# Edge groups from 22 on, not 29, take normalised source rows from a table; 13 groups of them as the node stage ends

## The reference, cut to what matters

```
h = relu(layernorm(x))                                  # every node
em = relu(layernorm([h[src], h[dst]] @ msg_w + msg_b) * msg_g + msg_beta) * edge_weight
messages = mean of em over the edges with the same target (0 where there is none)
gate = sigmoid(h @ gate_w + gate_b)
h_new = relu(layernorm([h, messages] @ upd_w + upd_b) * upd_g + upd_beta)
out = x + gate * h_new + (1 - gate) * h
```

## Time and profile before

| | us |
|---|---|
| median of three runs | 986.97 |
| lowest and highest run | 982.22, 993.64 |
| the profiled execution | 981.87 |
| its span, first to last instruction | 980.1 |

### The profile page before, as it was taken

How to read it: one execution, slowest core, us unless ns; L and a number is a source line. 1 busy time by engine, 2 the same in 40 slices (tenths; PEclk the granted TensorE clock), 3 DMA queues, 4 the chain that set the end, 5 groups by cost and what they waited for, 6 DMA issues and landing times.

```text
span 980.1 us, 19229 instructions
## 1 busy us (share of the span) xinstructions
PE 698.9 (71%) x3696; PEld 547.5 (56%) x3696; DVE 873.4 (89%) x3834; ACT 852.0 (87%) x3678; POOL 673.0 (69%) x602
## 2 busy tenths in 40 slices
PE   2377787877777777886766377777867878687781
PEld 1255555555555555554555266666756766576661
DVE  7299999999989999999995379999998888879984
ACT  3299999999989999999996389999989888779963
POOL 4667777776876877878747566766766666666557
PEclk9655655565555555556567698999899889889976
DMA  5246666666666667667523112333221111111111
GB/s 150 90 147 216 203 215 218 204 222 204 227 223 213 215 219 239 222 220 237 174 67 103 51 43 88 97 98 97 77 75 65 64 59 62 65 64 60 57 70 34
DMA packets 74260, 133.65 MB, mean 136 GB/s; under 512 B 15846, under 2 KB 17718, under 8 KB 74194
## 3 DMA queue, kind: packets, MB, share of 16 engines
q1 hardware_dynamic: 53868, 97.58, 28.6%
q0 software_dynamic: 18912, 34.84, 13.0%
q10 hardware_dynamic: 1414, 0.53, 0.2%
HBM read 56.01 MB, written 80.81 MB: 140 GB/s over the span
## 4 chain that ended last, share of the span: by engine, by line
ACT 45%; DVE 23%; issue 12%; PE 9%; another core or an unknown queue 6%; POOL 3%; ACTq 1%; DVEq 0%; DMA 0%; POOLq 0%; SPq 0%
ACT junk L410 13%; ACT hrow L403 9%; ACT work L437 8%; DVE work L458 5%; DVE work L469 5%; ACT xload L403 4%; POOL out L615 3%; DVE work L480 3%; ACT lnv L385 3%; DVE st L357 3%; ACT work L1134 2%; DVE work L475 2%; ACT rs L390 2%; PE pm L1273 2%
## 5 line engine op out<-in xcount | busy, mean ns | idle before, releaser
L615 POOL DMA_INDIRECT out<-work,sidx x196 | 201.4, 1027 | 128.0 <-issue 55.0
L1221 PE MATMUL pt<-ident,hrow 128*128 128x128 f32 x508 | 128.3, 401 | 128.9 <-ACT hrow L403 108.8
L610 POOL DMA_INDIRECT ring<-in_x,gidx x140 | 171.0, 1221 | 60.7 <-issue 41.1
L437 ACT ACTIVATE work<-work,gt 128x128 f32<-128x128 f32 x588 | 200.7, 413 | 3.7 <-DVE work L475 3.3
L1255 PE MATMUL py<-w_u,work 128*128 128x129 f32 x784 | 200.0, 434 | 0.0
L1255 PEld LDWEIGHTS py<-w_u,work 128*128 128x128 f32 x784 | 171.6, 322 | 39.2 <-issue 39.2
L610 POOL DMA_INDIRECT ring<-in_x,src_i x116 | 143.0, 1233 | 46.4 <-issue 34.4
L1221 PEld LDWEIGHTS pt<-ident,hrow 128*128 128x128 f32 x508 | 84.8, 202 | 159.3 <-ACT hrow L403 135.6
L410 ACT ACTIVATE junk<-py 128x128 bf16<-128x128 f32 x588 | 152.5, 278 | 18.5 <-remote 14.0
L469 DVE SCALAR_TENSOR_TENSOR work<-py,rs,g_upd 128x128 f32<-128x128 f32 x588 | 162.9, 336 | 4.2 <-ACT rs L390 4.2
L403 ACT ACTIVATE hrow<-xload,nb,rs 128x128 f32<-128x128 f32 x392 | 161.9, 489 | 3.0 <-DVE nb L396 2.7
(11 more groups left out here) (172 smaller groups left out, 1631.9 us busy)
## 6 DMA issues: line engine op xcount, KB each, us to landing
xload<-in_x SPq DMA_DIRECT2D x98, 256.0 KB
normalised_rows<-hrow SPq DMA_DIRECT2D x98, 256.0 KB
out<-work SPq DMA_DIRECT2D x98, 256.0 KB
running_sums<-acc SPq DMA_DIRECT2D x49, 256.0 KB
staged_target_rows<-work SPq DMA_DIRECT2D x14, 256.0 KB
ring<-staged_target_rows SPq DMA_DIRECT2D x14, 256.0 KB
out<-work,sidx POOLq DMA_INDIRECT x196
ring<-in_x,gidx POOLq DMA_INDIRECT x140
```

What stands on the lines that cost most here:

```text
L437: last = nc.scalar.activation(t_buf[:, g.at % 4, k, :], t_buf[:, g.at % 4, k, :], ACT.Relu, scale=gt[:, g.at % 4, k:k + 1])
L610: pool.indirect_dma_start(out=dest, out_offset=None, in_=rows, in_offset=bass.IndirectOffsetOnAxis(ap=idx, axis=0), **({} if rows is sums_ ...
L615: pool.indirect_dma_start(out=out, out_offset=bass.IndirectOffsetOnAxis(ap=idx, axis=0), in_=rows, in_offset=None, **if_tail).then_inc(s, 16)
L1221: last = nc.tensor.transpose(dest[:, k * H:(k + 1) * H], rows[:, k, :], ident[:, :])
```

## The change

Two constants change. Group 22 is now the first late group, and thirteen late groups (22 to 34) are gathered at the node stage's end, where there were ten (29 to 38).

```diff
 EARLY = 5
-LATE = 29
-UPFRONT = 10
+LATE = 22
+UPFRONT = 13
 REFILLED = 36
```

## The result

The changed kernel takes 1029.16 us, the median of four runs (1025.74 to 1035.29), beside 990.31 us for the kernel before on the same chip. The ratio is 1.0428 with the interval 1.0331 to 1.0525: it is slower. The profiled execution is the longest of the four, 1035.29 us with a span of 1033.2, so the two profiles stand 53.1 us apart, while the medians stand 38.9 apart.

A forecast was written before the change was run, and what follows sets the result against it. POOL's transfer issues, holding PE's signals, were taken to pace the edge stage. Refills +22, row of gathers +18, node stage -1 and savings 0 gave +39 us: 1021 by the profile, 1023 as median, range 1002 to 1037.

The forecast's parts named there:

- Refills, +22: Edge stage, groups 1 to 35: 16 more refill issues at 1.45 us each cost +22 us, bounds 21 and 26.
- before and after group 22 alike: Sign on POOL: groups with six issues come 9.4 to 9.7 us apart, no different before or after group 22.
- POOL never gets ahead again: Rival, edge stage: signals held over two groups after the long row, 1.5 us more per group, 1075 us; chance 0.04.
- The tell named for ACT: Sign in edge steps 23 to 43: ACT idles 2 us or more before line 1134 where six are issued.
- ACT's and DVE's savings, 0: Edge stage: seven groups lose normalisations and statistics, at best 8.4 us, taken as 0 since POOL's loop is longer.
- The rival in which these engines set the pace: Edge steps 23 to 29: ACT and DVE set the pace, POOL's transfers are hidden; 970 us, chance 0.07.
- The row of 52 gathers, +18: Node stage's end: 52 gathers in a row instead of 36 hold PE's signals longer, +18 us, between 9 and 24.
- The rival of the pipeline's filling: Node stage's end: 52 gathers in a row cost no more than 36, only refills cost; 1005 us, chance 0.17.
- The rival in which gains and losses cancel: Edge stage and node stage's end: refills cost 8 us, the row 9, savings offset them; 987 us, chance 0.07.
- The node stage, -1: Node stage: 28 fewer gathers on POOL, mostly off the path, give -1 us, between 0 and -4.

The follow-up runs named there:

- after again: The changed kernel's unchanged text run once more, beside the kernel before on another chip: ratio 1.0387 (1.0318 to 1.0455), span 1029.1 us.
- before again: The kernel before, its text unchanged, run once more for a second trace: ratio 0.9987 (0.995 to 1.0024), span 986.3 us.

## Why the prediction was right, step by step

**The direction and the size.** 1023 was forecast, 1029.16 was measured; +39 us was the sum, and the medians differ by 38.9. Of the two large terms one was good and one too small by the profiles, which differ by 53.1 and 42.8. So the direction and the mechanism were right, but that the sum meets the difference of the medians to 0.1 us is luck. The step from the sum to 1023 isn't exact either: with the median 5.1 us above the profiled execution it should have been 1026.

**Refills, +22: right.** The stretch was to take near 331 us and took 333.7 and 330.0. The loop of 1.45 us per issue and 0.85 us per group carried over from 191 issues to 207, and to 218 in the kernel with ten groups ahead (345.9 by the sum, 352.0 measured). Most six-issue groups in a row lose nothing extra. But "before and after group 22 alike" fails for groups 22 to 27: in after they take 61.0 us, where the loop's sum for their 35 issues gives 55.9. Twice there POOL goes from one group to the next without a pause, and ACT then waits about 5 us for PE's report (818.38, and 858.81 with 5.49):

```profile
809.41 1.03 POOL L615 DMA_INDIRECT out<-work,sidx  x1 [0.31 <-issue]
...
818.38 0.28 ACT L410 ACTIVATE junk<-pm 128x128 bf16<-128x128 f32 x1 [4.75 <-remote]
```

That is what the rival "POOL never gets ahead again" described, in two places and not over the whole stretch; its 1075 us did not come. Both places are there in after again as well (groups 22 and 26). Taking the refills out gave 57 us with the change and 21 without it. The tell named for ACT holds in part only: the wait ahead of line 1134 is 2.33 us at 751.42 in after, but 0.77 at 722.90, before group 22, where ACT still normalises and is itself later.

**ACT's and DVE's savings, 0: right.** The bound of 8.4 us was there as 11.5 once the refills were gone. As long as they stayed nothing of it shows: the stretch grew by about what the issues alone cost. The rival in which these engines set the pace needed late groups with six issues under 8.6 us; most came at 9.5, and the one at 8.3 follows one of 11.6. It is refuted.

**The row of 52 gathers, +18: too small.** The row ended at 579.8, where 578.4 was forecast. ACT was released at 584.97, not at 580 to 581, and from there to the first scatter it took 16.6 us (601.6 - 585.0), not the 9.2 that were read from before. Together 12.1 us. The step that failed is this last one: I carried the 9.2 us over as if the pipeline would stand at the same place when it is let go. It stood one step earlier. DVE's line 942 in after:

```profile
541.70 0.68 DVE L942 SCALAR_TENSOR_TENSOR acc<-acc,cont_wb 128x512 f32<-128x512 f32 x1
595.78 0.68 DVE L942 SCALAR_TENSOR_TENSOR acc<-acc,cont_wb 128x512 f32<-128x512 f32 x1
605.27 0.68 DVE L942 SCALAR_TENSOR_TENSOR acc<-acc,cont_wb 128x512 f32<-128x512 f32 x1
```

The same line in before, of which the fence shows the steps between 541 and 573 us:

```profile
553.15 0.68 DVE L942 SCALAR_TENSOR_TENSOR acc<-acc,cont_wb 128x512 f32<-128x512 f32 x1
572.50 0.67 DVE L942 SCALAR_TENSOR_TENSOR acc<-acc,cont_wb 128x512 f32<-128x512 f32 x1
```

The first scatter of either kernel falls 3 to 4 us ahead of the sixth of these (569.70 and 572.50; 601.58 and 605.27). In before, a signal came through in the middle, so the fifth ran at 553.15, inside the row; in after the fifth had to wait for the release, and both steps lay behind it. How many signals come through inside a row varies: after again had its release at 558.79 and its first scatter at 597.0. So this term is 18.5 us in one pair (597.0 - 578.5, before again to after again) and 31.9 in the other (601.6 - 569.7), the node stage's own difference included; 18 was the low edge of it.

**The rival of the pipeline's filling** (1005 us) said that a row of 52 costs no more than one of 36. Refuted: without the row the first scatter comes 55 us earlier, and ACT's work does not stop, its longest wait between 508 and 600 us being 1.57 us. The rival in which gains and losses cancel (987 us) is refuted by the result, since the interval of the ratio begins at 1.0331.

**The node stage, -1: not settled.** The two pairs give +1.8 and -2.8 us, and the stage's end varies between 520 and 539 us among kernels whose node stage is alike or nearly so.

**The skill's rule.** The Trainium skill (SBUF — State Buffer, "Who interferes with whom") has a DMA never contend with a compute engine. The prediction read that as saying that nothing would be held, and set it beside the rival of 970 us. The section speaks of the ports of SBUF and not of semaphores, so that reading went too far. The runs agree with the rule as far as the transfers' data go: with pauses, the same transfers moved at 82 GB/s beside an ACT that was busy 49.40 us of 58. What a row of issues on POOL did was to hold back PE's report by 49 us; the measurement decides here. As for "Rules for kernel authors" (DMA: Bandwidth & Descriptors), to issue early and wait late: 52 issues ahead of the first scatter cost 55 us, since they stand in POOL's order and each is an issue of 1.30 us.

**What stays open.** That the issues hold PE's signals is shown by the pair of memsets and gathers and by the pauses. By what path they hold them isn't. It isn't PE's report alone: ACT's was late once by 6.1 us (after again), though in the first profile of after ACT and DVE reported on time. Why the first long freeze sometimes lets a signal through after 23 us and sometimes after 37 isn't known either, nor is the shortest pause that helps; only one of 0.33 us was tried. And pauses changed little between refills: groups 1 to 8, with six issues and two pauses, come 8.7 to 9.1 us apart, but from group 10 on most take 9.5 again, so most of the refills' cost remained (323.4 us for the stretch, 333.7 and 330.0 without the pauses). Why groups 22 to 27 run into one another is open as well.

## What to carry to other kernels

When the chain names "an unknown queue" ahead of an engine, look up when its producer was recorded as done, and then what POOL was issuing at the time: three rows showed here that an engine idle a third of the time set the pace. Count POOL's indirect issues per step (here 1.45 us each and 0.85 per group) before trading compute for gathers; a saving on the engines that look full is worth nothing as long as that sum is above their step. And where a row of gathers is needed at a boundary of stages, keep it short and break it, here by a memset of 0.33 us, with a wait for it, after every second one; that and seven groups instead of thirteen gave the fastest version that does the whole work, 0.9676 of the kernel before.

## What the runs showed of the hardware that was not expected

- PE's signals to ACT were held for as long as 49 us after the recorded end of the instruction (535.48 to 584.97) while POOL issued 52 indirect transfers 1.30 us apart. A row of 156 memsets over 58 us, each with a wait for it, held nothing.
- PE itself slowed during the row: four transposes came one at a time with gaps of 0.3 to 1.1 us that the trace puts down to issue, and a little later PE stopped, waiting for ACT. After again, such gaps reach 3.12 us.
- A memset of 0.33 us and the wait for it after every second issue were enough in after: the longest wait on ACT in the row fell from 37.29 to under 5 us (4.98).
- A row no longer than before can hold longer: 23.95 us in the kernel with late groups from 22 and 10 ahead, 12.03 at most in the kernel before run again, both with 40 gathers.
